# Moving VectorE's side work and half of the query and key projections to other places of a batch

## The reference

```python
q, k, v = x @ Wq.T, x @ Wk.T, x @ Wv.T             # 16 heads; q, k have 16 channels a head, v has 64
k_enc, v_enc = x[:, :128] @ Wk_enc.T, x[:, :128] @ Wv_enc.T
f(x) = [1, x/2, (x outer x)/(4 sqrt 2)]            # Taylor features of exp
A = tril(f(q) f(k)^T);  A2 = f(q) f(k_enc)^T
out = (A v + A2 v_enc) / (row sums of both)        # z: one inverse for each head and token
x = layernorm(x + out @ Wout.T)
top1 expert of 8 by x @ wr + br;  x = layernorm(x + gate * (gelu(x w1 + b1) w2 + b2))
```

## Time and profile before

| | |
|---|---|
| median of 3 executions | 1218.67 us (1215.61 to 1218.83) |
| the profiled execution | 1217.28 us, span 1215.5 us |
| PE, PEld busy | 1080.9 us (89%), 629.5 us (52%) |
| DVE, ACT, POOL busy | 627.7 us (52%), 495.5 us (41%), 592.4 us (49%) |
| PE's granted clock, mean | 0.933 of full speed |

### The profile page before, as it was taken

The page is one execution under the profiler, slowest core; times in us unless marked ns, Lnnn a source line. Parts: engine busy times, 40 slices in busy tenths (PEclk is TensorE's granted clock), DMA queues, the critical chain, the costliest instruction groups (busy, mean ns, idle before and its releaser), DMA issues. The chain is left out here.

```text
span 1215.5 us, 16762 instructions
## 1 busy us (share of the span) xinstructions
PE 1080.9 (89%) x5296; PEld 629.5 (52%) x5297; DVE 627.7 (52%) x986; ACT 495.5 (41%) x868; POOL 592.4 (49%) x571
## 2 busy tenths in 40 slices
PE   5789899999989989989998998883479999999994
PEld 4344455445436445445544543463357766677663
DVE  5476864583492574466448349646423334343342
ACT  2557554544553454454454455300023233332331
POOL 1467755573574565456457357500124544444442
PEclk9789999999999899999999998976589999999998
DMA  6635352443534235235244343014551000111010
GB/s 205 249 108 183 92 193 83 142 152 118 155 120 161 92 114 218 102 91 184 85 150 148 122 131 92 1 35 169 226 237 33 31 33 29 34 35 31 25 31 2
DMA packets 54110, 134.90 MB, mean 111 GB/s; under 512 B 5854, under 2 KB 10176, under 8 KB 51746
## 3 DMA queue, kind: packets, MB, share of 16 engines
q1 hardware_dynamic: 50306, 124.81, 29.7%
q0 software_dynamic: 3744, 9.31, 2.5%
HBM read 87.73 MB, written 47.29 MB: 111 GB/s over the span
## 5 line engine op out<-in xcount | busy, mean ns | idle before, releaser
L379 ACT ACTIVATE w<-slot 128x1024 f32<-128x1024 f32 (+1 forms) x256 | 233.4, 915 | 176.3 <-PE slot L725 173.6
L339 POOL TENSOR_TENSOR wsum<-w 128x1024 f32<-128x1024 f32 x64 | 158.9, 2483 | 258.6 <-DVE w L493 258.6
L490 DVE SCALAR_TENSOR_TENSOR w<-w,mask 128x256 f32<-128x256 f32 (+1 forms) x192 | 192.9, 1005 | 169.6 <-ACT w L379 158.9
L746 PE MATMUL osum<-w,values 128*64 128x512 f32 (+3 forms) x1280 | 264.1, 511 | 2.0 <-DVE w L493 1.9
L342 POOL TENSOR_TENSOR wsum<-wsum,w 128x768 f32<-128x768 f32 x64 | 126.6, 1978 | 59.6 <-DVE w L493 59.6
L1156 ACT ACTIVATE active<-upT,b 128x128 f32<-128x128 f32 x312 | 84.9, 383 | 158.4 <-PE upT L1234 158.4
L1210 PE MATMUL down<-w,active 128*128 x624 | 144.2, 385 | 2.5 <-ACT active L1156 2.5
L1222 PE MATMUL up<-w,rowsT 128*128 x312 | 143.3, 603 | 0.7 <-ACT rowsT L1145 0.7
L725 PE MATMUL slot<-qop,kop 64*128 64x512 f32 (+3 forms) x640 | 130.2, 438 | 10.5 <-issue 8.3
L493 DVE TENSOR_SCALAR w<-w 128x768 f32<-128x768 f32 (+2 forms) x192 | 138.8, 723 | 0.0
L1210 PEld LDWEIGHTS down<-w,active 128*128 128x128 f32 x624 | 117.6, 193 | 18.7 <-issue 3.8
(11 more groups left out here) (186 smaller groups left out, 1215.9 us busy)
## 6 DMA issues: line engine op xcount, KB each, us to landing
kop<-k_rows SPq DMA_DIRECT2D x32, 640.0 KB, 4.7
qop<-q_rows SPq DMA_DIRECT2D x32, 512.0 KB, 5.9
w<-in_w SPq DMA_DIRECT2D x16, 1024.0 KB, 9.5
inv<-inv_rows SPq DMA_DIRECT2D x56, 256.0 KB, 5.7
k_rows<-kh SPq DMA_DIRECT2D x32, 320.0 KB
k_rows<-kl SPq DMA_DIRECT2D x32, 320.0 KB
q_rows<-qh SPq DMA_DIRECT2D x32, 256.0 KB
q_rows<-ql SPq DMA_DIRECT2D x32, 256.0 KB
```

What stands on the lines that cost most here:

```text
L339: pool.tensor_tensor(dst, src[:, :, 0:N], src[:, :, N:2 * N], ALU.add).then_inc(wsummed, 1)
L379: act.activation(w[:, n % 2, :, at:at + cols], slot[u % 2][:, :, 0:cols], ACT.Square, bias=HALF_ROOT).then_inc(squared, 1)
L490: dve.scalar_tensor_tensor(src[:, :, 0:cut], src[:, :, 0:cut], 0.5, mask[:, 0:cut].unsqueeze(1).to_broadcast([P, 2, cut]), ALU.add, ALU.mu ...
L746: last = pe.matmul(osum[n % 2][HD * s:HD * s + HD, q0:N], values[:, j, h * HD:h * HD + HD], w[:, n % 2, s, at:at + N - q0], start=(u == 0) ...
```

## The change

The tables move the pieces: late values from gaps 0 to 4 to gaps 0, 1, 3, 5, 6; the first three query and key projections one gap later, the last two from gaps 15 and 17 to gaps 25 and 27; the output pieces from 18, 20, 22, 24 to 15, 17, 19, 21; the early values, the turned rows and the router three, three or two, and one gap earlier. The high part of the input and the copies of the turned rows pass from VectorE to ScalarE. The low part stands in gap 8 (was 7). The eight normalisations stand in gaps 4, 5, 6, 7, 9, 10, 12, 13 (were 8 to 15). Moments, deviation and centring stand in gaps 22, 23 and 24 (were 25, 26, 27). The logits are read in gap 31, not in gap 0 of the next batch. SyncE issues the first half of the inverse's loads ahead of the third gather, and the sending of heads 8 to 15 after the normalised rows of the batch before are stored.

```diff
-V_LATE_AT = {0: 0, 1: 1, 2: 2, 3: 3, 4: 4}
-QK_AT = {9: 0, 11: 1, 13: 2, 15: 3, 17: 4}
+V_LATE_AT = {0: 0, 1: 1, 3: 2, 5: 3, 6: 4}
+QK_AT = {10: 0, 12: 1, 14: 2, 25: 3, 27: 4}
...
-INVERT_GAP, NORM_GAP, MOMENTS_GAP, CENTRE_GAP, RSTD_GAP = 1, 8, 25, 27, 26
+NORM_AT = {4: 0, 5: 1, 6: 2, 7: 3, 9: 4, 10: 5, 12: 6, 13: 7}
+INVERT_GAP, MOMENTS_GAP, CENTRE_GAP, RSTD_GAP = 1, 22, 24, 23
...
+            def split_x_high(b):
+                act.wait_ge(xT_loaded, 16 * (b + 1))
+                act.wait_ge(piece_full, nth(b - 1, "v", 9) + 1)
+                act.activation(xh[:, :, :], xT[:, :, :], ACT.Copy).then_inc(x_split, 1)
+
+            def copy_turned(b, k):
+                act.wait_ge(piece_full, nth(b, "turn", k) + 1)
+                bank = osum[1] if b == B - 1 and k == 1 else piece
+                act.activation(yT[:, 4 * k:4 * k + 4, :], bank[:, :].rearrange("p (t n) -> p t n", n=P),
+                               ACT.Copy).then_inc(piece_read, 1)
...
-            def split_x_high(b):
-                dve.wait_ge(xT_loaded, 16 * (b + 1))
-                dve.wait_ge(piece_full, nth(b - 1, "v", 9) + 1)
-                dve.tensor_copy(xh[:, :, :], xT[:, :, :]).then_inc(x_split, 1)
...
-                    if b > 0 and 0 <= g - NORM_GAP < PAIRS:
-                        normalise((b - 1) * PAIRS + g - NORM_GAP)
+                    if b > 0 and g in NORM_AT:
+                        normalise((b - 1) * PAIRS + NORM_AT[g])
```

More of the change, by code:

```diff
@@ L38 @@
 RING, ATT, INV = 4, 14, 4
-V_LATE_AT = {0: 0, 1: 1, 2: 2, 3: 3, 4: 4}
-QK_AT = {9: 0, 11: 1, 13: 2, 15: 3, 17: 4}
-OUT_AT = {18: 0, 20: 1, 22: 2, 24: 3}
-V_EARLY_AT = {19: 0, 21: 1, 23: 2, 25: 3, 27: 4}
-TURN_AT, ROUTER_AT = {29: 0, 30: 1}, 31
-XH_GAP, XL_GAP = 6, 7
-INVERT_GAP, NORM_GAP, MOMENTS_GAP, CENTRE_GAP, RSTD_GAP = 1, 8, 25, 27, 26
+V_LATE_AT = {0: 0, 1: 1, 3: 2, 5: 3, 6: 4}
+QK_AT = {10: 0, 12: 1, 14: 2, 25: 3, 27: 4}
+OUT_AT = {15: 0, 17: 1, 19: 2, 21: 3}
+V_EARLY_AT = {16: 0, 18: 1, 20: 2, 22: 3, 24: 4}
+TURN_AT, ROUTER_AT = {26: 0, 28: 1}, 30
+XH_GAP, XL_GAP = 7, 8
+NORM_AT = {4: 0, 5: 1, 6: 2, 7: 3, 9: 4, 10: 5, 12: 6, 13: 7}
+INVERT_GAP, MOMENTS_GAP, CENTRE_GAP, RSTD_GAP = 1, 22, 24, 23
 COPY_UNIT, DEN_UNIT = 0, 3
@@ L277, in _ @@
                     store_inverse(b - 1)
+                if b > 0:
+                    for g in range(2):
+                        load_inverse(b - 1, g)
                 gather(b, 2)
                 if b > 0:
-                    for g in range(PAIRS // 2):
+                    for g in range(2, PAIRS // 2):
                         load_inverse(b - 1, g)
@@ L285, in _ @@
                     gather(b + 1, 0)
-                    send(b + 1, 1)
                 if b > 0:
@@ L289, in _ @@
                 if b + 1 < B:
+                    send(b + 1, 1)
                     gather(b + 1, 1)
@@ L440, in _ @@
                         copy_values(b + 1, 0, V_EARLY_AT[g - 1])
+                    if b > 0 and g - 1 in TURN_AT:
+                        copy_turned(b - 1, TURN_AT[g - 1])
+                    if b + 1 < B and g == XH_GAP:
+                        split_x_high(b + 1)
                     if b * PAIRS + p + 1 < B * PAIRS:
@@ L448, in _ @@
             copy_att(B * PAIRS - 1)
+            copy_turned(B - 1, 0)
+            copy_turned(B - 1, 1)
         @block.vector
@@ L465, in split_v, with split_x_low @@
                 dve.tensor_tensor(lo, src, hi.bitcast(F32), ALU.subtract).then_inc(w_split, 1)
-            def split_x_high(b):
+            def split_x_low(b):
                 dve.wait_ge(xT_loaded, 16 * (b + 1))
-                dve.wait_ge(piece_full, nth(b - 1, "v", 9) + 1)
-                dve.tensor_copy(xh[:, :, :], xT[:, :, :]).then_inc(x_split, 1)
-            def split_x_low(b):
                 dve.wait_ge(x_split, 2 * b + 1)
@@ L543, in centre @@
                                       ALU.mult).then_inc(y_ready, 1)
-            def copy_turned(b, k):
-                dve.wait_ge(piece_full, nth(b, "turn", k) + 1)
-                bank = osum[1] if b == B - 1 and k == 1 else piece
-                dve.tensor_copy(yT[:, 4 * k:4 * k + 4, :],
-                                bank[:, :].rearrange("p (t n) -> p t n", n=P)).then_inc(piece_read, 1)
             def logits_of(b):
@@ L582, in _ @@
                         residual(b - 1, OUT_AT[g - 1])
-                    if b > 0 and g - 1 in TURN_AT:
-                        copy_turned(b - 1, TURN_AT[g - 1])
-                    if b > 1 and g == 0:
-                        logits_of(b - 2)
+                    if b > 0 and g - 1 == ROUTER_AT:
+                        logits_of(b - 1)
                     if n < B * PAIRS and u > 0:
                         finish_weights(n, u)
-                    if b + 1 < B and g == XH_GAP:
-                        split_x_high(b + 1)
                     if b + 1 < B and g == XL_GAP:
@@ L600, in _ @@
                         centre(b - 1)
-            logits_of(B - 2)
             invert(B - 1)
@@ L612, in _ @@
             centre(B - 1)
-            copy_turned(B - 1, 0)
-            copy_turned(B - 1, 1)
             logits_of(B - 1)
```

## The result

| | before | after |
|---|---|---|
| median (executions) | 1218.22 us (4; 1215.61 to 1218.83) | 1185.32 us (4; 1180.53 to 1187.41) |
| ratio | | 0.9728, 95% interval 0.9696 to 0.9761 |
| the profiled execution, its span | 1217.28, 1215.5 us | 1187.41, 1185.7 us |
| PE's granted clock, mean | 0.933 | 0.942 |

The account below looks back on a forecast made before the run. TensorE, busy 89%, loses some 10 us a batch to waits and lower clock, partly because VectorE and GpSimd block each other. 6 x (3.1 + 0.5 + 0.2) + 2 + 6 = 30.8 off 1217.28: 1186.5, median 1188, range 1178 to 1198.

Parts of the forecast that it names:

- point 1: Turned rows, batches 1 to 6: late projections and early values cover the centring chain; gain 3.1 us a batch.
- point 2: Router: with a bare gap behind and no idling just ahead, less lower clock; gain 0.5 us a batch.
- point 3: Gap 5 to first output piece, batches 1 to 6: VectorE's and GpSimd's work adds up to 25.2 us; gain 0.2 each.
- point 5: Batch 0, without normalisations: low part needed one gap later and the cast gone; gain 2 us, bounds 1 to 4.
- point 6: Last batch: first output piece 4.2 us late instead of 8.4, gain 4; shorter wait at turned rows, gain 2.
- The lighter stretch: Rival: VectorE and GpSimd don't add up as taken, or the inverse is there in time; 1168 us, chance 0.15.
- The rival of queueing: Inverse's store queues behind second gather, rows and input, so the inverse comes late; 1201 us, chance 0.17.
- the late bound: Latest expected landing of the inverse's second load, 17.7 us after gap 0's start; 15.9 was forecast.
- G + 20.3: Inverse's landing after gap 0's start that uses up the gain; rival of a landing at 22: 1231 us, chance 0.10.
- ScalarE's copies: High part on ScalarE costs nothing, its 0.68 us off VectorE counted in the stretch; turned copies nothing, -0.3 to +0.3.
- The rivals that end above the forecast: Late inverse (1201 us, chance 0.17), far later inverse (1231, 0.10), waits only moved (1214 to 1221, 0.06).
- The waits were not only moved: Rival: turned rows' gain is lost to pieces waiting for low parts and a longer stretch; 1214 to 1221 us, chance 0.06.

Follow-up runs that it names:

- e3: Kernel before the change with only the last two query and key projections moved, to gaps 26 and 28: 1205.59 us, ratio 0.9910.
- e5: Changed kernel with the last early value piece in gap 29 instead of 24, between turned rows and router: 1182.87 us, ratio 0.9714.
- e4: Changed kernel with all eight loads of the inverse behind the third gather, as before the change: 1203.77 us, ratio 0.9894.
- e9: Changed kernel with the next input's load issued behind the first four loads of the inverse: 1179.60 us, ratio 0.9680.
- e10: Changed kernel with the next input's load behind the inverse's first four loads and the inversion in gap 0 instead of 1: 1175.03 us, ratio 0.9649.
- e11: The kernel of e10 with the last early value piece also moved, from gap 24 to 29: 1179.18 us, ratio 0.9674.
- e6: Changed kernel with GpSimd adding only 32 columns a half from the third pair on, denominators left incomplete: 1139.35 us, ratio 0.9342.
- e1: Changed kernel with the eight normalisations in gaps 5, 6, 7, 9, 10, 11, 12, 13, the first behind the finish part: 1185.85 us, ratio 0.9727.
- e2: Changed kernel with the input's high part and the copies of the turned rows back on VectorE: 1186.93 us, ratio 0.9739.
- e7: Changed kernel with the low part of the input in gap 7 instead of 8: 1186.53 us, ratio 0.9749.

## Why the prediction was right, point by point

The forecast was 2.7 us off (1188 against 1185.3). The main mechanisms were found, but several sizes were wrong, by up to 6.7 us, and cancelled. That the total came so close is luck in that measure:

| us of span gained | forecast | measured |
|---|---|---|
| point 1, turned rows | 18.6 | 19.1 |
| point 2, router's lower clock | 3.0 | -3.7 |
| point 3, gap 5 to the first output piece | 1.2 | 6.4 |
| point 5, batch 0 | 2 | 4.1 |
| point 6, last batch and what follows | 6 | 3.9 |
| sum | 30.8 | 29.8 |

The measured column is from one execution of each kernel. Point 6 is what the other rows leave of the span's 29.8: 4.5 us up to the last batch's inverse, worked out below, less 0.6 in all that follows.

1. Turned rows: right in cause and size, and e3 shows that the late projections do it. The chain took 9.5 us, 2.7 shorter than the one I kept for safety, but not for the reason I gave: the wait for GpSimd in it was still there (2.67 us). The turned pieces' wait for a low part, costed at nothing, is nothing here; with a piece more ahead of it (e5) it is 0.3 to 0.5, a little more than the 0.3 I had as its most.

2. The router: this step failed. I took it that with no idling ahead of it the lower clock would come less often. It cost more in this execution (table, 7.0 to 10.7). The first row below is of the end of the third batch in the changed kernel, at the full clock; the others are of the end of the fourth, with the same denominators at the lower one:

```profile
305.44 0.64 PE L763 MATMUL den<-wsum,onehot 128*32 128x256 f32 x8
...
396.62 1.95 PE L716 MATMUL piece<-wr,yT 128*128 128x8 f32 x16
...
399.83 1.08 PE L763 MATMUL den<-wsum,onehot 128*32 128x256 f32 x8
400.85 0.79 PE L729 MATMUL slot<-qop,kop 64*128 64x512 f32 x2
```

The granted clock was 1.00 from 386 to 398.5 us and 0.58 from there to 401. PE was busy for 9.89 of the 10 us from 386 to 396, and none of its rows in them or in the router has an idle time. Idling just ahead of the router isn't needed for it.

3. The stretch: its length held nearly to the tenth. From gap 5's finish part to the output piece 25.1 to 25.2 us pass (25.2 forecast) in 31 of the 36 batches 1 to 6 of the changed kernel, e4, e5, e9, e10 and e11, wherever it starts, and e6 shows the cause, the two engines holding each other up. The landing was taken 1.3 us too late for most batches. The store was as forecast (issued from G + 7.28 to 8.58), but the loads followed it 1.06 us later and not 2.06, since the third gather is no longer issued between them; the rest is the landing. Over six batches the first normalisation ran at a mean of G + 15.2, and the gain is 1.1 a batch, my upper bound, not 0.2. Gap 15 begins 23.1 to 24.4 us behind the first normalisation in every one of them, and e4 confirms the price of a later one. What the prediction missed is the other side: an inverse that comes earlier gains little (e1, e11). The finish part of gap 5 can't start at G + 13.75, as I carried over from the old table, but only at 14.8, for it then waits for ScalarE, an engine that my sum of the stretch left out. The changed kernel is at 14.8 to 15.2 in four of six batches. The lighter stretch (1168) asked for the sum not to hold, and it does, or for the inverse to be in time: e11 has that, and its output piece is still 3.9 us behind e6's, where 2.9 was supposed.

The rival of queueing is the nearest to have happened. Where the input was issued behind G, the inverse's loads came later, by 1.2 us in the fourth batch and by 3.3 in batch 1; of the 3.3, 1.5 are the store's own lateness, which was there before the change. In batch 1 the first normalisation was at G + 17.6, near the late bound. The Trainium skill, "DMA: Bandwidth & Descriptors", section "Two DMAs through the same engine are not ordered", has descriptors of one queue start in order; the loads at G + 9.63 and 10.80, with the store at G + 7.28 in both, agree. The first normalisation never came near G + 20.3, from which the change would have lost.

4. ScalarE's copies: the cast is in the sum, and e2 agrees (5.5 us more of waiting in seven batches, 0.8 each, where the cast is 0.68). The turned copies are nothing, as costed.

5. Batch 0: 4.1 us, the upper bound, in this execution; with e1's batch 0, which is the same in its code, it would be 1.2. At the first projection itself 3.2 are gained, since the lower clock behind the wait was shortened along with the wait, which my 2 left out; the rest lies in gaps 5 to 8, where the executions of one and the same batch 0 differ (in e1 PE waits 2.02 us there for VectorE's weights, in the changed kernel 0.62 for GpSimd's sum).

6. The last batch. Its first output piece and its turned rows, which answer to the earlier trace rows (G = 686.68):

```profile
722.93 5.48 PE L673 MATMUL piece<-wo,att 128*128 128x256 f32 x16 [0.36 <-DVE att L519]
...
757.81 1.09 PE L709 MATMUL piece<-ident,y 128*128 128x128 f32 x4 [2.38 <-DVE y L559]
```

The piece came at G + 36.25 (35.6 forecast, 31.4 undisturbed), so 4.9 late against 8.4 before: a gain of 3.5 there, 4 forecast. The turned rows wait 2.38 us and not 6.04, 3.7 less. But from the first output piece to the logits' end I find 49.0 us here (722.93 to 771.92, where the wait for the inverse of the last batch ends) and 45.6 before (756.70 to 802.27), with three gaps, 4.4 us, more in it: a gain of 1.0 and not 3.7. 1.8 of the missing 2.7 is in the first row: the 16 matmuls take 5.48 us, 3.69 in the earlier trace rows, for the clock has fallen behind the waits just ahead of them; where the other 0.9 went I haven't found. Where 16 gaps stand without slack ahead of the piece, a wait is paid for once more in the piece behind it, and my sum had no term for that.

The rivals that end above the forecast are out. The inverse was near its late bound in one batch only. The waits were not only moved: the turned rows' gain stands in full (e3 has it alone) and nothing of it came back in the stretch.

## What to carry to other kernels

Where VectorE and GpSimd each look half idle, add their work up over the stretch that ends at a needed result, and move the work and not the wait: e1 and e7 took away waits and won nothing, e6 took away the work and was 4% faster. Of a step moved earlier, ask what it then waits for and what else stands in that queue: half of the inverse's loads issued ahead of a gather were worth 18 us of this kernel (e4). The same thought applied once more, to the input and the inversion, found little left in the stretch (1.4 us of e10's gain), since another engine, ScalarE, came next. Fill PE's wait for a chain with pieces that nobody needs soon, which was the largest part here (19 us).

## What the runs showed of the hardware

- An addition of GpSimd stretches VectorE's instruction from 0.81 to 2.75 us (512 columns, mask) and from 1.35 to 2.28 (1024 columns, subtraction). The Trainium skill, "SBUF — State Buffer", section "Who interferes with whom", says that an instruction of VectorE with two inputs in SBUF contends with one of GpSimd that reads SBUF. Both of these have two such inputs, and the rows agree.
- PE's lower clock behind the router came without an idle time ahead of it, in some batches and executions and not in others (granted clock 0.58 in 398.5 to 401 us of the changed kernel, 1.00 at the same place one batch earlier): between 0.0 and 10.7 us a profiled execution over these kernels. Executions of one kernel with the higher mean clock are mostly the shorter ones (e4: 1195.43 us at 0.948, 1207.70 at 0.936). What decides it is open.
- The inverse's store (four transfers of 8 KB) and the loads that wait for it are issued 2.35 us apart where what was issued ahead of the store had time to land, and up to 5.75 us where a gather, the rows or the input were issued shortly before it (3.5 in the changed kernel's fourth batch, 4.55 in e10's third). The store's place in time is then a poor guide to when its reader starts.
